# Gated cross-attention and mixture-of-experts attention: gates ahead of the scales, and the weights split in three turns, in the kernel's head

## The reference

```
x = x + tanh(g_xattn) * xattn(ctx, layernorm(x), Wk, Wq, Wv)   # softmax over 77 context tokens, one head of 128
x = x + tanh(g_ffn)   * ffn(layernorm(x), ...)

ffn(h):
  logits = normalised(h) @ normalised(sim_matrix) - sigmoid(gates)      # 16 experts
  w      = softmax over the experts with logits > 0 (the best two where none is)
  q, k, v = sum over e of w[:, e] * (h @ proj[e])     for q_proj, k_proj, v_proj: (16, 128, 128)
  o      = softmax(q k^T / sqrt(128)) v               # within a sequence
  out    = sum over e of w[:, e] * (o @ o_proj[e])
```

## Time and profile before

| | |
|---|---|
| time, median of 3 runs | 800.66 us (800.41 to 801.44) |
| time of the profiled execution | 799.99 us |
| its span, first to last instruction | 798.1 us |
| TensorE busy | 776.1 us (97%) |
| VectorE busy | 607.2 us (76%) |
| GpSimd busy | 483.0 us (61%) |
| ScalarE busy | 433.8 us (54%) |
| mean granted clock of TensorE | 0.987 of full speed |

### The profile page before, as it was taken

The page is one execution under the profiler, slowest core; times in us unless marked ns, Lnnn a source line. Parts: engine busy times, 40 slices in busy tenths (PEclk is TensorE's granted clock), DMA queues, the critical chain, the costliest instruction groups (busy, mean ns, idle before and its releaser), DMA issues.

```text
span 798.1 us, 13995 instructions
## 1 busy us (share of the span) xinstructions
PE 776.1 (97%) x3999; PEld 418.1 (52%) x3999; DVE 607.2 (76%) x2037; ACT 433.8 (54%) x1129; POOL 483.0 (61%) x703
## 2 busy tenths in 40 slices
PE   7489999999999999999999999999999999999998
PEld 6445545555455555545555554555555455544444
DVE  2977787878787787778777787877878786775648
ACT  5554645556555655655565565456556555544445
POOL 3276657674746757474675747567574755765534
PEclk9789999999999999999999999999999999999999
DMA  6564476563655636365563636546364654543100
GB/s 192 136 216 159 162 219 174 169 209 94 209 161 164 189 106 204 97 210 167 151 191 106 202 109 209 166 150 186 101 207 116 208 160 139 163 135 116 53 14 28
DMA packets 97476, 122.57 MB, mean 154 GB/s; under 512 B 14611, under 2 KB 69111, under 8 KB 97399
## 3 DMA queue, kind: packets, MB, share of 16 engines
q1 hardware_dynamic: 96679, 121.59, 49.6%
q10 hardware_dynamic: 720, 0.08, 0.1%
HBM read 97.32 MB, written 24.31 MB: 152 GB/s over the span
## 4 chain that ended last, share of the span: by engine, by line
PE 88%; DVE 5%; DMA 2%; POOL 1%; ACT 1%; issue 1%; SPq 0%; DVEq 0%; ACTq 0%; POOLq 0%
PE acc_q L1380 20%; PE acc_k L1380 20%; PE acc_v L1380 20%; PE y L1409 9%; PE oT_p L1409 9%; PE m L1489 2%; PE m L1553 2%; DVE x_all L1175 1%; PE oT_p L1641 1%; PE m L1480 1%; PE m L1539 1%; DMA stage<-in_L_ffn_q_proj_dram 1%; PE m L1469 1%; POOL zq L658 1%; PE m L1529 1%
## 5 line engine op out<-in xcount | busy, mean ns | idle before, releaser
L658 POOL TENSOR_TENSOR zq<-zq_full,zq 128x512 f16<-128x512 f32 x256 | 297.8, 1170 | 222.4 <-ACT zq L743 222.2
L743 ACT ACTIVATE zq<-zq_full 128x512 f16<-128x512 f32 x256 | 160.1, 636 | 224.1 <-DVE zq_full L1145 224.0
L1175 DVE SCALAR_TENSOR_TENSOR x_all<-y,w_out,x_all 128x128 f32<-128x128 f32 x356 | 122.2, 343 | 96.1 <-issue 69.5
L1380 PE MATMUL acc_q<-zq,w_hi 128*128 128x512 f16 x510 | 193.3, 379 | 1.0 <-POOL zq L658 1.0
L1380 PE MATMUL acc_k<-zq,w_hi 128*128 128x512 f16 x510 | 193.2, 379 | 0.0
L1380 PE MATMUL acc_v<-zq,w_hi 128*128 128x512 f16 x510 | 193.2, 379 | 0.0
L1145 DVE TENSOR_TENSOR zq_full<-wq_bc,x2T_p 128x512 f32<-128x512 f32 x256 | 167.8, 668 | 2.5 <-DMA wq_bc<-w_rows 1.7
L1175 DVE SCALAR_TENSOR_TENSOR x_all<-oT_p,w_out,x_all 128x128 f32<-128x128 f32 x356 | 121.5, 341 | 0.0
L673 POOL TENSOR_TENSOR x_all<-stage,x_all 128x128 f32<-128x128 f32 x240 | 100.4, 456 | 19.8 <-DVE x_all L1175 13.3
L1380 PE MATMUL acc_q<-zq,w_lo 128*128 128x512 f16 x255 | 96.6, 379 | 0.0
L1380 PE MATMUL acc_v<-zq,w_lo 128*128 128x512 f16 x255 | 96.6, 379 | 0.0
(11 more groups left out here) (253 smaller groups left out, 1091.4 us busy)
## 6 DMA issues: line engine op xcount, KB each, us to landing
wq_bc<-w_rows SPq DMA_DIRECT2D x128, 512.0 KB, 4.5
blk_rows<-stage SPq DMA_DIRECT2D x26, 256.0 KB, 2.7
stage<-blk_rows SPq DMA_DIRECT2D x104, 64.0 KB, 2.0
blk_rows<-v_blk SPq DMA_DIRECT2D x15, 256.0 KB, 2.0
v_mix<-blk_rows SPq DMA_DIRECT2D x60, 64.0 KB, 2.9
blk_rows<-pc_blk SPq DMA_DIRECT2D x15, 256.0 KB, 4.1
pcT<-blk_rows SPq DMA_DIRECT2D x60, 64.0 KB, 2.0
out_dram<-x_all SPq DMA_DIRECT2D x15, 256.0 KB, 6.7
```

What stands on the lines that cost most here:

```text
L658: nc.gpsimd.tensor_tensor(zq[:, 1, e % Z_SLOTS, :], zq_full[:, e % F_SLOTS, :], zq[:, 0, e % Z_SLOTS, :], ALU.subtract).then_inc(zq_lo_poo ...
L743: nc.scalar.activation(zq[:, 0, e % Z_SLOTS, :], zq_full[:, e % F_SLOTS, :], ACT.Copy).then_inc(zq_hi_done, 1)
L1175: nc.vector.scalar_tensor_tensor(out=rows(x_all, g, b0 + b), in0=bank[:, tok(j)], scalar=w_out[:, g % 2, e, b0 + b:b0 + b + 1], in1=rows(x ...
L1380: last = nc.tensor.matmul(acc[m][:], w[:, m, s, :], zq[:, half, s % Z_SLOTS, :], start=(s == 0 and n == 0), stop=(s == E - 1 and n == 2))
```

## The change

On SyncE, head() no longer waits for the projections, sends q's weights first, then the context of groups 1 to 3, k's weights, x, v's weights and the rest; the first expert's gates go in a DMA of their own (256 KB, semaphore wq_first_in), the second's in another.

On VectorE, v's maximum and the scales stand behind the gates of group 0. The weights' high and low parts are made in three turns: experts 0 to 3, 4 to 9, 10 to 15 (PARTS). The first turn lies ahead of the first expert's products, the second among experts 1 to 3, the third inside body(0): at s = 6 on ScalarE, at s = 8 on VectorE. TensorE waits for a turn's parts at experts 0, 4 and 10.

On TensorE, px_transpose(0) moves ahead of the transposes of the contexts 2 and 3, att_product(0) ahead of the products for group 1, the gathering of the maxima behind the scores of group 1; keep_busy counts are changed. On ScalarE, x2_norm(1) moves from body(0) into the head, and on GpSimd second_rstd(1) one expert ahead.

```diff
@@
+PARTS = ((0, 4), (4, 10), (10, 16))
@@
+        def split_part(t, m, part):
+            experts = slice(*PARTS[part]) if m < O else slice(0, E)
+            return t[:, m, experts].rearrange("p e h -> p (e h)")
@@ sync, head
-                sp.wait_ge(kq_in, 16 * 2)
+                load_weights(Q, q_proj)
                 sp.dma_start(zq_full[0:S, 0:PRE].rearrange("p k (b c) -> p (k b) c", b=G),
                              c_v[:, G:G * (PRE + 1), :]).then_inc(ctx_pre_in, 16)
-                load_weights(Q, q_proj)
                 load_weights(K, k_proj)
+                load_x(1)
                 load_weights(V, v_proj)
-                load_x(1)
                 load_weights(O, o_proj)
                 load_x(2)
                 weight_rows(0)
-                for j in range(W_SLOTS):
+                for e, done in enumerate((wq_first_in, wq_in[0])):
+                    src = w_rows[0:1, G * e:G * (e + 1), :].rearrange("a r n -> (a r n)")
+                    sp.dma_start(wq_bc[:, 0, e], src.partition_broadcast(P)).then_inc(done, 16)
+                for j in range(1, W_SLOTS):
                     spread_q(0, j)
@@ gpsimd, head
-                for e in range(LEAD - 1):
+                for e in range(LEAD - 2):
                     zq_low(0, e)
                 second_rstd(1)
-                zq_low(0, LEAD - 1)
+                for e in (LEAD - 2, LEAD - 1):
+                    zq_low(0, e)
@@ scalar
-            def weight_high(m):
+            def weight_high(m, part=0):
                 act.wait_ge(scales_done, 1 if m < O else 2)
-                nc.scalar.activation(w_hi[:, m], stage[:, m], ACT.Copy,
+                nc.scalar.activation(split_part(w_hi, m, part), split_part(stage, m, part), ACT.Copy,
                                      scale=w_up[:, m:m + 1]).then_inc(hi_done[m], 1)
@@ scalar, head
-                ctxT_out(1)
                 pxT_out(0)
-                ctxT_out(2)
-                ctxT_out(3)
-                kxT_out(1)
-                vx_out(1)
-                for g in range(2, PRE + 1):
+                for g in range(1, PRE + 1):
+                    ctxT_out(g)
+                for g in range(1, PRE):
                     kxT_out(g)
                     vx_out(g)
                 x2_norm(0)
+                kxT_out(PRE)
                 x2T_out(0)
-                weight_high(Q)
+                vx_out(PRE)
+                x2T_move(0)
                 x_norm(1)
                 gate_exps(0)
                 xnT_out(1)
-                x2T_move(0)
+                x_exps(1)
+                weight_high(Q)
+                pxT_out(1)
                 weight_high(K)
-                x_exps(1)
-                pxT_out(1)
                 weight_high(V)
-                for e in range(LEAD):
-                    zq_high(0, e)
+                zq_high(0, 0)
+                weight_high(Q, 1)
+                weight_high(K, 1)
+                zq_high(0, 1)
+                weight_high(V, 1)
+                zq_high(0, 2)
+                x2_norm(1)
+                zq_high(0, 3)
@@ scalar, body
-                    if s == 1 and i < 2:
+                    if s == 1 and i == 1:
                         x2_norm(g2)
...
+                    if i == 0 and s == 6:
+                        for m in (Q, K, V):
+                            weight_high(m, 2)
@@ vector (weight_low(m, part=0) waits for hi_done[m] at part + 1 and works on split_part)
@@ vector, zq_scale
-                if e % 2 == 0:
+                if (g, e) == (0, 0):
+                    dve.wait_ge(wq_first_in, 16)
+                elif e % 2 == 0 or (g, e) == (0, 1):
@@ vector, head
                 weight_max(K)
+                first_stats(1)
                 setup_gate()
-                weight_max(V)
-                share_largest(0)
-                first_stats(1)
-                weight_scales(0)
                 x2_norm_inverse(0)
                 gate_logits(0)
                 gate_mask(0)
                 gate_softmax(0)
+                weight_max(V)
+                x_max(1)
+                share_largest(0)
+                weight_scales(0)
                 weight_low(Q)
-                x_max(1)
                 weight_low(K)
                 x_sum(1)
                 zq_scale(0, 0)
+                weight_low(V)
                 zq_scale(0, 1)
-                weight_low(V)
-                zq_scale(0, 2)
                 x1_add(1)
                 second_stats(1)
+                zq_scale(0, 2)
+                weight_low(Q, 1)
+                weight_low(K, 1)
                 zq_scale(0, 3)
+                weight_low(V, 1)
                 first_stats(2)
@@ vector, body
+                    if i == 0 and s == 8:
+                        for m in (Q, K, V):
+                            weight_low(m, 2)
@@ tensor, experts
+                    for part, (first, _) in enumerate(PARTS):
+                        if (i, s) == (0, first):
+                            pe.wait_ge(hi_done[m], part + 1)
+                            pe.wait_ge(lo_done[m], part + 1)
@@ tensor, head
                 vx_product(0)
+                ctx_transpose(1)
+                px_transpose(0)
+                for g in range(2, PRE + 1):
+                    ctx_transpose(g)
+                att_product(0)
                 for g in range(1, PRE + 1):
-                    ctx_transpose(g)
-                px_transpose(0)
-                kx_product(1)
-                att_product(0)
-                vx_product(1)
-                for g in range(2, PRE + 1):
                     kx_product(g)
                     vx_product(g)
                 pe.wait_ge(kxT_sb, 3)
-                keep_busy(8)
+                keep_busy(6)
                 x2_transpose(0)
-                pe.wait_ge(vx_sb, PRE + 1)
-                gather_max(0, acc[V])
                 pe.wait_ge(prep_dve, 4)
                 for b in range(G):
                     small_product(-1, 4, b)
-                spread_max(0, acc[K])
                 xn_transpose(1)
                 for b in range(G):
                     small_product(-1, 9 - sooner(-1), b)
+                keep_busy(3)
+                pe.wait_ge(vx_sb, PRE + 1)
+                gather_max(0, acc[V])
+                spread_max(0, acc[K])
+                keep_busy(2)
                 px_transpose(1)
+                keep_busy(2)
                 att_product(1)
+                keep_busy(2)
```

More of the change, by code:

```diff
@@ L269, in flamingo_gated_moe_attention @@
         w_rows_in = sem("w_rows_in")
+        wq_first_in = sem("wq_first_in")
         wq_in = [sem(f"wq_in{k}") for k in range(W_SLOTS)]
@@ L1064, in weight_scales, with weight_low @@
                     nc.vector.tensor_scalar(out_scale[:], out_scale[:], tanh_f[:], None, ALU.mult).then_inc(scales_done, 1)
-            def weight_low(m):
-                dve.wait_ge(hi_done[m], 1)
+            def weight_low(m, part=0):
+                dve.wait_ge(hi_done[m], part + 1)
                 nc.vector.scalar_tensor_tensor(
-                    out=w_lo[:, m].rearrange("p e h -> p (e h)"), in0=stage[:, m].rearrange("p e h -> p (e h)"),
-                    scalar=w_up[:, m:m + 1], in1=w_hi[:, m].rearrange("p e h -> p (e h)"),
-                    op0=ALU.mult, op1=ALU.subtract).then_inc(lo_done[m], 1)
+                    out=split_part(w_lo, m, part), in0=split_part(stage, m, part), scalar=w_up[:, m:m + 1],
+                    in1=split_part(w_hi, m, part), op0=ALU.mult, op1=ALU.subtract).then_inc(lo_done[m], 1)
             def blocks_transposed(dst, src, done):
```

## The result

The changed kernel is slower: 804.02 us, median of 5 runs (803.96 to 805.01), against 800.66 (799.98 to 801.44) in the same five rounds; the ratio is 1.0044 [1.0031, 1.0058]. That is 1.5 us above the range of 797.6 to 802.5. The profiled execution took 804.0, its span 802.2, against 799.99 and 798.1. One caution for what follows: within one kernel the experiments' executions lie up to 3.5 us apart (801.3 to 804.2 over ten of one of them, 803.6 to 807.1 over four of another), so where two kernels differ by 1 or 2 us I go by the places in their profiles.

A forecast was written before the change was run, and what follows sets the result against it. TensorE hardly runs dry from expert 4 on, so a head edit is worth what it moves the dense part left. Sum -3.4 + 0.8 + 2.6 + 0.5 - 0.84 = -0.34 us, forecast 800.3, range 797.6 to 802.5.

The forecast's parts named there:

- G: Gain at expert 4's start, released by GpSimd: 51.05 instead of 54.43, so 3.4 us.
- d: Cost of second-turn low parts on VectorE meeting GpSimd's second_rstd(1): 0 to 1.6 us, taken as 0.8.
- Step 1: Loads: q's weights sent without the wait land at 11.4; cost taken as 0, up to 1.5 if small loads slow.
- step 2: Head, px transposed first: x1_add(0) at 17.4 instead of 19.02, 1.6 earlier; logits end at 26.05.
- Step 3: Gates first: w_blk at 30.6 instead of 34.40; first broadcast issued 3.0 later, no longer what ends last.
- Step 4: Scales last, before the first product: w_up at 35.3, first expert at 39.3 instead of 43.21, gain 3.9.
- Step 5: Experts 1 to 4: GpSimd's serial chain sets the pace; expert 4 at 51.05 instead of 54.43.
- Step 6: VectorE and GpSimd collisions at the second turn's low parts: one wait, 0.8 us, between 0 and 1.6.
- Step 7: Third turn in body(0): VectorE 2.6 us plus collisions of 0.5 later, 0.84 hidden; px_transpose(2) waits for x_exps(2).
- c: Cost of third-turn low parts meeting GpSimd's zq_low(0,12): 0.2 to 1.3 us, taken as 0.5.
- (B): Rival: every possible VectorE and GpSimd port collision occurs, d = 1.6 and c = 1.3; 801.9 to 802.7; chance 0.20.
- (C): Rival: q's weights in front of the small loads make G smaller by up to 1.5; 801.8; chance 0.08.

The follow-up runs named there:

- k6: Changed kernel with loads in the order of before and q's maximum behind second_stats(0) on VectorE; 802.73 us, ratio 1.0027 to the kernel before.
- k1_wait_back: Changed kernel with SyncE's wait for the two projections back in front of q's weights; 806.6 us, ratio 1.008 to the kernel before.

## Why the prediction was wrong

Sizes first: the forecast was -0.34 = -3.4 (G) + 0.8 (d) + 2.26 (third turn). Measured on the span: G is 54.43 - (42.17 + 11.79) = 0.47; the collisions and the clock are 2.11; the stretch of the third turn is 2.37; with 0.09 behind it, +4.1. G is that of the changed kernel's one profile, whose head is the earliest of six alike; with the others' it would be 0.1 to -1.0.

**Step 1 failed, and with step 2 it is 2.07 of the 4.4 missed.** I set the cost of q's early load at 0, with ScalarE's x_norm(0) as cover and 1.5 as the upper end. It was 1.4 at the projections, and the kernel before with that load alone was 0.2% slower. The cover was wrong: x_norm(0) can hide nothing of it, as it stands behind the copy of the projection on its own engine, and behind sig, which waited 1.44 longer for the gates' load. What reached it was 1.04.

**Step 2 failed with it.** x1_add(0) at 19.35, not 17.4. About 1.1 is the loads (18.23 with q's in its old place; 1.4 on the mean of the profiles). The rest is TensorE's own products, 0.46 longer in the transposes and 0.35 in the scores, of which I had costed none. The granted clock is 0.76 and 0.50 there (8 to 12 and 12 to 16 us), 0.96 and 0.62 before; but in k6, with the old load, the transposes last 1.11 at a recorded 1.00, so that the clock is the cause isn't shown. From there to the logits the chain was right (8.77 against 8.65), but with the loads mended by q's maximum behind the statistics another term was due that I had not made: VectorE's own sum, busy till 27.15. So 26.05 was out of reach in that order. With q's maximum ahead of x1_add(0) VectorE had 2.11 to spare, but that needs q's weights early, and no run has them early at no cost.

**Step 3 was right.** Logits to w_blk 4.53 (4.5), first broadcast 2.87 later (3.0), zq_full not released by the DMA.

**Step 4 was right in kind, 0.75 short.** w_up came 4.60 + 0.17 behind w_blk (4.7), but the first product another 4.75 behind it (4.0). The turns last 0.72 and 0.75; between them VectorE waits 0.79 and 0.88 for ScalarE's high parts, whose second stands behind pxT_out(1), and that one waits 0.43 for TensorE. I had let it cost its own 0.6 only, with the keep_busy products at 0.2 each in TensorE's idle time. They don't all lie there: px was ready at 36.58, but two of them (36.44, 1.22 us at a clock of 0.50) stood ahead of px_transpose(1), which began at 37.45 and took 1.06.

**Step 5 was right**: 11.79 without collisions against 11.75, released by GpSimd.

**Step 6 was mis-sized, and lacked a term.** I took d = 0.8; it was 1.55, its upper end (1.6). The trace had shown one row for each end and I took the middle; what decides is which begins first and what it is. The row that spoke for 0 was VectorE entering GpSimd's root; in the new order it is GpSimd's small operations that meet VectorE's low part. That is what the Trainium skill says (SBUF — State Buffer, section "SBUF: two separate sides"): the one that starts first holds the pair of ports for its whole instruction, here 0.23 made 1.07 and 0.87; but its other half, GpSimd's root holding VectorE, the product sn of 0.17 contradicts. The lacking term is the clock, 0.57 at expert 4 and 1.13 in all: I looked only at which instruction comes last, not at what TensorE's clock may do after it stood 2.56 us.

**Step 7 was right in its waits, and its number is partly luck**: 2.37 against 2.26. The low parts alone are 2.9, not 2.6; c was 0.9 instead of 0.5; and 1.3 was hidden (3.80 less the 22.18 - 19.71 that the low parts cost) instead of 0.84, so the misses cancel. Of the 2.37, 0.55 is the trail of the late logits, which the step had not in it. px_transpose(2) waits for px by 0.98, the wait at expert 10 is 0.89, as foretold.

What came was rivals (B) and (C) at once. (C) came near its full price of 1.5, and (B)'s d at its own, with the clock's 0.57 on top; (B)'s c came only in part. I had priced each alone, with the rest as in the forecast, so the range stopped where one of them does: (C) 1.4 and then 1.4 of (B) and the clock add up to 803.1. Of the 4.4 missed on the span these are 2.5 to 2.8; the other 1.6 to 1.9 are TensorE's own products in step 2, the 0.75 of step 4 and small ones, which stood in no rival. Nothing made them exclude each other. And the bound that I should have worked out: the best of each stage as measured, 42.2 for the first product, 11.8 without the second low parts and 19.7 without the third, adds up to 73.7, against 74.24 before. With the stages as they ran here, even free of all collisions, the split has about half a microsecond to win, since what it takes from before the first product comes back before expert 4, where GpSimd's chain sets the pace. That is no bound on orders that weren't tried, and it is less than the spread of the head.

## What to carry to other kernels

Before you price an earlier start of a stage, find what sets the pace of the next one; work taken from ahead of the first product went into the stage of an engine chain that was already last. Cost each rival on top of the others, unless something makes them exclude each other. A large load sent while small ones that the first products need are still on their way delays these, though it stands behind them in the queue (projections 1.3 to 1.4 us later here). And before you say what a fix did to the clock, look for a run without the fix in which the clock did the same.

## What the runs showed of the hardware

- VectorE's low part (two inputs and an output in SBUF) holds up GpSimd operations that come while it runs: operations of 4 columns go from 0.23 to 1.07 and 0.87, the root from 1.04 to 1.65. The other way round it depends on the operation: GpSimd's products get between three low parts in a row and make 3.80 or 4.65 of 2.9, but its root, begun first, let a VectorE product of 0.17 pass.
- After a wait of 2.56 us the granted clock fell to 0.50 (1.2 GHz) only when TensorE was running again, at 52 to 54 us, in the middle of dense work. The same wait of 2.55 in k1_wait_back was followed by no fall. With ten unused fp32 products of 0.24 each in the wait it stayed at 1.00 in two of two profiles, one of which says nothing by the comparison above; twenty were too many.
- A 1 MB load issued at 2.8 us made the 64 KB load ahead of it in the same queue usable 1.4 later, and a load on ScalarE's queue 1.6 later (sim_sq at 9.06 instead of 7.45).
